# A mixture of experts: from every token through every expert to tokens sorted into 23 tiles of one expert each

## The chip, the cores and the metric

The kernel runs on one core of one Trainium2 chip. The metric is the device time of the program in microseconds (us). A core has TensorE (PE, matrix products), VectorE (DVE), ScalarE (ACT), GpSimd (POOL), SyncE (SP, here the issuer of DMAs), the on-chip memories SBUF and PSUM, and 16 DMA engines between SBUF and DRAM.

## The reference, cut to what matters

Two layers work on x of 2048 tokens of 128 values. The change touches only the last part, a mixture of experts with eight experts (H = 128, F = 512), of which each token wants the result of one:

```
hn2    = layernorm(x) * g + b                       # (2048, 128)
logits = hn2 @ gate_w + gate_b                      # (2048, 8)
idx    = argmax(logits, axis=-1)                    # one expert per token
mid    = relu(einsum('th,ehf->etf', hn2, w1) + b1[:, None, :])
y      = einsum('etf,efh->eth', mid, w2) + b2[:, None, :]
moe    = y[idx, arange(2048)]
return x + moe
```

All numbers are float32.

## The kernel before, in words

The program is a chain of stages, each a block in which every engine has its own list of instructions; `end_stage` frees the semaphores and lets all engines meet at a barrier. The two stages of the mixture come last, and after them one DMA writes the result (L1564).

`moe_prep_stage` normalises the 16 groups of 128 tokens (`xn`), transposes them on TensorE (L1413), scales and shifts them into `hn2` on ScalarE, forms the logits (L1418), and VectorE works out the one-hot choice `oh` (L1393 to L1401). TensorE then transposes `oh` (L1424) and multiplies it by `b2` (L1430), and VectorE adds that to the residual `S.res` (L1406).

`moe_stage` runs every token through every expert: 8 experts times 4 chunks of 512 tokens are 32 steps. A step has four products of 512 tokens with `w1` (`hidden`, L1508), four ScalarE relus (L1478), 16 products of 128 tokens with `w2` (`output`, L1517) and four VectorE instructions (L1491) that add the result times the column of `oh` to `S.res`, so that only the chosen expert counts. SyncE loads an expert's weights (256 KB for `w1`, 256 KB for `w2`, 2 KB for `b1`) into one of two buffers, two experts ahead. Nothing leaves SBUF until the end.

The order on each engine is the order in which the code is written; semaphores are the only link between engines. A float32 product on TensorE with a 128 x 128 weight shows as two matmul rows in the profile, a transpose as one.

Of the kernel before, what the change touches and what calls it, by code (L numbers as in the profile page):

```python
# [14 lines left out]
I32 = mybir.dt.int32  # L15
ALU = mybir.AluOpType
# [3 lines left out]
P = 128  # L20
# [12 lines left out]
NFB = NF // P  # L33
DI, NS, KC, DR = 256, 16, 4, 8
# [1283 lines left out]
def moe_prep_stage(nc, S, dr):  # L1318

    with ExitStack() as ctx:  # L1320
# [22 lines left out]
        @block.sync  # L1343
        def _(sp):
            sp.dma_start(gw[:, :], dr["gate_w"]).then_inc(w_load, 16)
            sp.dma_start(gb[:, :], dr["gate_b"]).then_inc(w_load, 16)
            sp.dma_start(b2[:, :], dr["b2"]).then_inc(w_load, 16)
            sp.wait_ge(w_load, 48)

        @block.gpsimd  # L1350
        def _(pool):

            pool.iota(rank_i[:, :], pattern=[[-1, NE]], base=NE, channel_multiplier=0).then_inc(rank_ready, 1)

        @block.scalar
        def _(act):
            act.wait_ge(var_ready, 1)
            act.activation(lnv[:, :], lnv[:, :], ACT.Ln).then_inc(act_c, 1)
            act.wait_ge(act_c, 1)
            act.activation(rstd[:, :], lnv[:, :], ACT.Exp, scale=-0.5).then_inc(rstd_ready, 1)  # L1360
            for c in range(NCH):
                act.wait_ge(xn_psum, c + 1)
                act.activation(S.hn2[:, c * CH:(c + 1) * CH], banks[c], ACT.Identity, bias=V("ln2_b"),
                               scale=V("ln2_g")).then_inc(hn_ready, 1)
            for c in range(NCH):
                act.wait_ge(ohT_psum, c + 1)
                act.activation(ohT[:, c * CH:(c + 1) * CH], banks[c][0:NE, :], ACT.Copy).then_inc(ohT_ready, 1)

        @block.vector
        def _(dve):  # L1370
# [18 lines left out]
            dve.wait_ge(rank_ready, 1)  # L1389
            link(dve.tensor_copy(rank[:, :], rank_i[:, :]))  # L1390
            dve.wait_ge(w_load, 48)
# [6 lines left out]
            link(dve.tensor_tensor(pick[:, :, :], pick[:, :, :], rank[:, :].unsqueeze(1).to_broadcast([P, NT, NE]),  # L1398
                                   ALU.mult))
            link(dve.tensor_reduce(top[:, :], pick[:, :, :], AX.X, ALU.max))  # L1400
            dve.tensor_tensor(S.oh[:, :, :], pick[:, :, :], top[:, :].unsqueeze(2).to_broadcast([P, NT, NE]),  # L1401
                              ALU.is_equal).then_inc(oh_ready, 1)
            for c in range(NCH):
                dve.wait_ge(b2_psum, c + 1)
                r = S.res[:, TPC * c:TPC * (c + 1), :]
                dve.tensor_tensor(r, r, banks[4 + c].rearrange("p (i d) -> p i d", d=P), ALU.add).then_inc(dve_c, 1)  # L1406

        @block.tensor
        def _(pe):
# [5 lines left out]
            pe.wait_ge(w_load, 48)  # L1415
            pe.wait_ge(hn_ready, NCH)
            for t in range(NT):
                mm = pe.matmul(banks[4][:, NE * t:NE * (t + 1)], S.hn2[:, P * t:P * (t + 1)], gw[:, :],  # L1418
                               start=True, stop=True)
            mm.then_inc(lg_psum, 1)  # L1420
            pe.wait_ge(oh_ready, 1)
            for c in range(NCH):
                for i in range(TPC):
                    mm = pe.transpose(banks[c][0:NE, P * i:P * (i + 1)], S.oh[:, TPC * c + i, :], S.ident[:, :])  # L1424
                mm.then_inc(ohT_psum, 1)
            for c in range(NCH):
                pe.wait_ge(ohT_ready, c + 1)
                for i in range(TPC):
                    t = TPC * c + i
                    mm = pe.matmul(banks[4 + c][:, P * i:P * (i + 1)], ohT[:, P * t:P * (t + 1)], b2[:, :],  # L1430
                                   start=True, stop=True)
                mm.then_inc(b2_psum, 1)


def moe_stage(nc, S, dr):

    with ExitStack() as ctx:
# [5 lines left out]

        w1, w2, b1 = sb("w1", [P, 2, NF]), sb("w2", [P, 2, NFB, P]), sb("b1", [P, 2, NFB])
        mid = sb("mid", [P, 2, NFB, CH])
        banks = S.banks
        w_load = [sem("w_load0"), sem("w_load1")]
        mid_psum, mid_ready, y_psum, added = sem("mid_psum"), sem("mid_ready"), sem("y_psum"), sem("added")
        block = ctx.enter_context(nc.Block())
        NP = NE // 2  # L1450

        @block.sync
        def _(sp):
            def load(e, par):
                sp.dma_start(w1[:, par, :], dr["w1"][bass.ds(e, 1)].rearrange("o h f -> h (o f)")).then_inc(w_load[par], 16)  # L1455
                sp.dma_start(w2[:, par, :, :], dr["w2"][bass.ds(e, 1)].rearrange("o (b p) h -> p (o b) h", p=P))\  # L1456
                    .then_inc(w_load[par], 16)
                sp.dma_start(b1[:, par, :], dr["b1"][bass.ds(e, 1)].rearrange("o p b -> p (o b)")).then_inc(w_load[par], 16)

            load(0, 0)  # L1460
            load(1, 1)
            with sp.Fori(0, NP - 1) as ep:
                for par in range(2):

                    sp.wait_ge(y_psum, ep * (2 * NCH) + (NCH * (par + 1) + 2))
                    load(ep * 2 + (2 + par), par)

        @block.scalar
        def _(act):
            with act.Fori(0, NP) as ep:  # L1470
                for par in range(2):
                    for c in range(NCH):
                        step = NCH * par + c

                        act.wait_ge(y_psum, ep * (2 * NCH) + (step + 1))
                        for f in range(NFB):
                            act.wait_ge(mid_psum, ep * (2 * NCH * NFB) + (NFB * step + f + 1))
                            act.activation(mid[:, c % 2, f, :], banks[f], ACT.Relu,  # L1478
                                           bias=b1[:, par, f:f + 1]).then_inc(mid_ready, 1)

        @block.vector
        def _(dve):
            dve.sem_inc(added, 2)
            with dve.Fori(0, NP) as ep:
                for par in range(2):
                    for c in range(NCH):
                        step = NCH * par + c
                        dve.wait_ge(y_psum, ep * (2 * NCH) + (step + 3))
                        for i in range(TPC):
                            t = TPC * c + i  # L1490
                            ins = dve.scalar_tensor_tensor(  # L1491
                                out=S.res[:, t, :], in0=banks[4 + c % 2][:, P * i:P * (i + 1)],
                                scalar=S.oh[:, t, bass.ds(ep * 2 + par, 1)], in1=S.res[:, t, :],
                                op0=ALU.mult, op1=ALU.add)
                        ins.then_inc(added, 1)
                        dve.wait_ge(added, ep * (2 * NCH) + (step + 3))

        @block.tensor
        def _(pe):
            pe.sem_inc(mid_ready, NFB)  # L1500
            pe.sem_inc(y_psum, 2)

            def hidden(ep, par, c):
                step = NCH * par + c
                for f in range(NFB):

                    pe.wait_ge(mid_ready, ep * (2 * NCH * NFB) + (NFB * step + f + 1))
                    pe.matmul(banks[f], w1[:, par, P * f:P * (f + 1)], S.hn2[:, c * CH:(c + 1) * CH],  # L1508
                              start=True, stop=True).then_inc(mid_psum, 1)

            def output(ep, par, c):
                step = NCH * par + c
                pe.wait_ge(added, ep * (2 * NCH) + (step + 1))
                pe.wait_ge(mid_ready, ep * (2 * NCH * NFB) + (NFB * (step + 2)))
                for i in range(TPC):
                    for f in range(NFB):
                        mm = pe.matmul(banks[4 + c % 2][:, P * i:P * (i + 1)], mid[:, c % 2, f, P * i:P * (i + 1)],  # L1517
                                       w2[:, par, f, :], start=(f == 0), stop=(f == NFB - 1))
                mm.then_inc(y_psum, 1)

            with pe.Fori(0, NP) as ep:
                for par in range(2):
                    for c in range(NCH):
                        if c == 0:
                            pe.wait_ge(w_load[par], ep * 48 + 48)
                        hidden(ep, par, c)
                        if par or c:
                            output(ep, *divmod(NCH * par + c - 1, NCH))
                output(ep, 1, NCH - 1)
# [92 lines left out]
```

## Time and profile before

| | |
|---|---|
| device time, median of 3 runs | 1865.42 us (1864.46 to 1867.36) |
| the profiled execution: its own time | 1863.32 us |
| its span, first to last instruction | 1861.5 us |
| preparation stage, first instruction to last | 1588.93 to 1622.22 us |
| expert stage, first weight load issued to last add | 1622.99 to 1855.74 us |
| last DMA, issue to end of span | 1856.62 to 1861.5 us |

The profiled execution's time is 1.8 us more than its span; a change of the span is added to that time. Lines of the profile name lines of the kernel (L1508), and tiles by their names without buffer numbers, so that `xe_w` is both `w1` and `w2`, and `x_hn` is `hn2`.

### The profile page before, as it was taken

The page shows a single profiled execution, that of the slowest core. Times are in us where ns is not written, and L with a number is a line of the kernel's source. Part 1 is how long each engine was busy: PE and PEld are TensorE (multiplying, and loading weights), DVE is VectorE, ACT ScalarE, POOL GpSimd, SP SyncE. Part 2 cuts the span into 40 slices and gives each one's busy share as a digit, 9 for nine tenths or more (in the row PEclk, how much of TensorE's full clock was granted, in tenths as well). Part 3 has the DMA queues.
Part 4 walks back from the last instruction along what each step waited for, and adds up shares of the span by engine and source line. Part 5 has one row for each costly group of instructions (what it writes and reads, how often), then busy time and mean ns, then how long its engine had stood idle before and what let it go on. Part 6 is the DMA issues. An engine that isn't in the chain of part 4 may idle for free. (4 is left out here: it accounts for less than half of the span.)

```text
span 1861.5 us, 19912 instructions
## 1 busy us (share of the span) xinstructions
PE 1271.1 (68%) x6752; PEld 472.7 (25%) x6752; DVE 1273.2 (68%) x1980; ACT 892.9 (48%) x1211; POOL 476.7 (26%) x433
## 2 busy tenths in 40 slices
PE   0432599999999999999690233349223334699998
PEld 0220022222222222222230000023000002467776
DVE  8934899999999999994301899960179997311111
ACT  2220077777777777778443344423434442244332
POOL 1200000000000000000002999940279996000000
PEclk6765599999999999999895555569555555699999
DMA  0011010001000000000006655500565560000000
GB/s 27 0 76 73 28 48 1 2 34 41 1 1 38 38 2 1 2 1 1 22 4 175 131 114 112 102 10 15 148 132 113 111 131 4 23 12 23 11 23 23
DMA packets 53271, 86.33 MB, mean 46 GB/s; under 512 B 7950, under 2 KB 18854, under 8 KB 53182
## 3 DMA queue, kind: packets, MB, share of 16 engines
q1 hardware_dynamic: 53182, 85.23, 18.6%
q8 instruction: 46, 0.75, 0.2%
q14 instruction: 43, 0.35, 0.1%
HBM read 71.81 MB, written 13.11 MB: 46 GB/s over the span
## 5 line engine op out<-in xcount | busy, mean ns | idle before, releaser
L653 DVE TENSOR_REDUCE at_mpart<-psum 128x1 f32<-128x512 f32 x1024 | 656.8, 686 | 48.5 <-PE psum L718 37.6
L632 ACT ACTIVATE at_probs<-psum 128x1024 f32<-128x1024 f32 x512 | 496.2, 1021 | 272.3 <-PE psum L743 272.1
L756 PE MATMUL psum<-at_probs,at_vg 128*32 128x512 f32 x2048 | 273.6, 606 | 0.4 <-ACT at_probs L632 0.4
L743 PE MATMUL psum<-at_qs,at_ks 75*128 75x512 bf16 x1024 | 269.7, 385 | 1.3 <-ACT at_probs L632 0.2
L714 PE MATMUL psum<-at_ks,at_qs 64*128 64x512 bf16 x512 | 207.9, 406 | 84.2 <-DMA at_km<-k_parts 49.9
L718 PE MATMUL psum<-at_km,at_qm 64*128 64x512 bf16 x512 | 208.0, 406 | 0.0
L608 POOL CAST at_m<-at_mneg 128x16 bf16<-128x16 f32 x16 | 3.1, 196 | 697.8 <-DVE at_mneg L658 697.8
L1491 DVE SCALAR_TENSOR_TENSOR res<-psum,x_oh,res 128x128 f32<-128x128 f32 x128 | 36.0, 344 | 197.5 <-PE psum L1517 197.5
L1239 PE MATMUL psum<-msf_hc,m_stack 128*32 128x512 f32 x256 | 60.1, 1027 | 161.1 <-DVE msf_hc L1164 151.9
L1239 PE MATMUL psum<-msb_hc,m_stack 128*32 128x512 f32 x256 | 59.9, 1024 | 160.8 <-DVE msb_hc L1164 151.8
L1220 POOL TENSOR_TENSOR msb_inject<-msb_dus,msb_bs 128x512 f32<-128x512 f32 x128 | 160.6, 1319 | 26.9 <-DMA msb_cs<-m_bc 26.9
L1220 POOL TENSOR_TENSOR msf_inject<-msf_dus,msf_bs 128x512 f32<-128x512 f32 x128 | 159.7, 1299 | 27.2 <-DMA msf_cs<-m_bc 27.2
L1478 ACT ACTIVATE xe_mid<-psum,xe_b 128x512 f32<-128x512 f32 x128 | 87.9, 687 | 145.1 <-PE psum L1508 145.1
L714 PEld LDWEIGHTS psum<-at_ks,at_qs 64*128 64x128 bf16 x512 | 47.7, 93 | 384.3 <-DVE at_mpart L653 331.1
L1517 PEld LDWEIGHTS psum<-xe_w,xe_mid 128*128 128x128 f32 x1024 | 118.8, 192 | 13.4 <-issue 13.4
L1508 PE MATMUL psum<-x_hn,xe_w 128*128 128x512 f32 x256 | 117.6, 606 | 5.5 <-DMA xe_b<-in_b 5.5
L1517 PE MATMUL psum<-xe_w,xe_mid 128*128 128x128 f32 x1024 | 118.8, 275 | 0.0
L743 PEld LDWEIGHTS psum<-at_qs,at_ks 75*128 75x128 bf16 x1024 | 78.2, 98 | 135.4 <-issue 52.0
L1148 ACT ACTIVATE psum<-msf_dts,m_aneg 128x512 f32<-128x512 f32 x128 | 85.5, 686 | 47.4 <-DVE msf_hp L1191 19.1
L1148 ACT ACTIVATE psum<-msb_dts,m_aneg 128x512 f32<-128x512 f32 x128 | 85.5, 686 | 47.0 <-DVE msb_hp L1191 19.1
L1191 DVE TENSOR_TENSOR_SCAN psum<-psum,msf_last,msf_inject 128x512 f32<-128x512 f32 x66 | 84.6, 1318 | 0.0
L1191 DVE TENSOR_TENSOR_SCAN psum<-psum,msb_last,msb_inject 128x512 f32<-128x512 f32 x66 | 84.3, 1313 | 0.0
(240 smaller groups left out, 1311.4 us busy)
## 6 DMA issues: line engine op xcount, KB each, us to landing
msf_dts<-m_dt SPq DMA_DIRECT2D x32, 256.0 KB
msf_dus<-m_dtu SPq DMA_DIRECT2D x32, 256.0 KB
msb_dts<-m_dt SPq DMA_DIRECT2D x32, 256.0 KB
msb_dus<-m_dtu SPq DMA_DIRECT2D x32, 256.0 KB
at_qs<-q_parts SPq DMA_DIRECT2D x48, 96.0 KB
at_ks<-k_parts SPq DMA_DIRECT2D x48, 96.0 KB
msf_bs<-m_bc SPq DMA_DIRECT2D x16, 256.0 KB
msf_cs<-m_bc SPq DMA_DIRECT2D x16, 256.0 KB
```

What stands on the lines that cost most here:

```text
L632: act.activation(probs[:, u % 2, p, :], s_pair[p], ACT.Exp, scale=float(HD) ** -0.5).then_inc(probs_ready, 1)
L653: dve.reduce_max(mpart[:, s % 2, 2 * jp + b, i, kc:kc + 1], ring[x % 3], AX.X).then_inc(ring_free, 1)
L714: pe.matmul(ring[x % 3], S.qs[0:HALF, buf, q], S.ks[0:HALF, buf, k], start=True, stop=True)\
L718: pe.matmul(ring[y % 3], S.qm[64:64 + HALF, buf, q], S.km[64:64 + HALF, buf, k], start=True, stop=True)\
L743: mm = pe.matmul(s_banks[p][b], S.ks[0:DM, g % 2, j * T + kt * P:j * T + (kt + 1) * P], S.qs[0:DM, g % 2, j * T + c * CH:j * T + (c + 1) * ...
L756: mm = pe.matmul(o_bank[VW * j:VW * (j + 1), :], vg[:, g % 2, kt, j, :], probs[:, u % 2, j // 2, CH * (j % 2):CH * (j % 2 + 1)], start=(kt ...
L1148: act.activation(decay[k % ND], dts[:, i % 2, j, :], ACT.Exp, scale=S.aneg[:, n:n + 1]).then_inc(decay_ready, 1)
L1191: dve.tensor_tensor_scan(h, decay[k % ND], inject[:, k % NI, :], before if c else 0.0, ALU.mult, ALU.add).then_inc(scanned, 1)
L1220: pool.tensor_tensor(inject[:, k % NI, :], dus[:, i % 2, j, :], bs[:, c % 2, q, :], ALU.mult).then_inc(injected, 1)
L1239: mm = pe.matmul(y_bank[i % 2][GC * j:GC * (j + 1), :], S.stack[:, :], hc[:, r % 2, j, :], start=False, stop=(q == NQ - 1), tile_position= ...
L1508: pe.matmul(banks[f], w1[:, par, P * f:P * (f + 1)], S.hn2[:, c * CH:(c + 1) * CH], start=True, stop=True).then_inc(mid_psum, 1)
L1517: mm = pe.matmul(banks[4 + c % 2][:, P * i:P * (i + 1)], mid[:, c % 2, f, P * i:P * (i + 1)], w2[:, par, f, :], start=(f == 0), stop=(f == ...
```

## The change

The expert stage no longer takes every token through every expert. The preparation stage works out, for each token, a row in a list sorted by expert, in which each expert starts at a new tile of 128 rows; `NSLOT` = 16 + 8 - 1 = 23 tiles hold any choice. The normalised tokens are scattered to `x_dram` in DRAM, one indirect DMA on POOL's queue for each of the 16 groups; before that a plain DMA fills `x_dram` with zeros. The product of the one-hot choice with `b2` is gone from this stage. `eid` is the expert of each tile. The expert stage then walks over the 23 tiles: SyncE loads the tile's 128 rows of `x`, reads the expert's number from SBUF into a register, and loads `w1`, `b1`, `w2` and `b2` from that expert's address (`W` = 3 buffers); TensorE transposes `x`, multiplies by `w1`, then a row of ones by `b2` and the hidden values by `w2`; ScalarE evicts; SyncE stores the 128 result rows to `y_dram`. When all 23 are stored, POOL gathers them by 16 indirect DMAs, and VectorE adds them to `S.res`. The loops over experts are now written out.

The core of the diff (declarations, and lines that only rename, are left out):

```diff
@@ moe_prep_stage, sync @@
-            sp.dma_start(b2[:, :], dr["b2"]).then_inc(w_load, 16)
-            sp.wait_ge(w_load, 48)
+            sp.wait_ge(zeros_ready, 1)
+            sp.dma_start(S.x_dram.rearrange("(s p) d -> p s d", p=P),
+                         zeros[:, :].unsqueeze(1).to_broadcast([P, NSLOT, P])).then_inc(zeroed, 16)
+            sp.wait_ge(w_load, 32)
@@ gpsimd @@
+            pool.wait_ge(zeroed, 16)
+            pool.wait_ge(pos_ready, 1)
+            for i in range(NT):
+                pool.indirect_dma_start(S.x_dram, bass.IndirectOffsetOnAxis(ap=S.pos[:, i:i + 1], axis=0),
+                                        xn[:, i, :], None).then_inc(scattered, 16)
+            pool.wait_ge(scattered, 16 * NT)
@@ scalar @@
-            for c in range(NCH):
-                act.wait_ge(ohT_psum, c + 1)
-                act.activation(ohT[:, c * CH:(c + 1) * CH], banks[c][0:NE, :], ACT.Copy).then_inc(ohT_ready, 1)
@@ vector @@
-            for c in range(NCH):
-                dve.wait_ge(b2_psum, c + 1)
-                r = S.res[:, TPC * c:TPC * (c + 1), :]
-                dve.tensor_tensor(r, r, banks[4 + c].rearrange("p (i d) -> p i d", d=P), ALU.add).then_inc(dve_c, 1)
+            dve.wait_ge(counts, 1)
+            link(dve.tensor_tensor_scan(upto[:, :, :].rearrange("p e i -> p (e i)"),
+                                        first[:, :, :].rearrange("p e i -> p (e i)"), of_tile, 0.0, ALU.mult, ALU.add))
...
+            link(dve.tensor_reduce(posf[:, :], rank[:, :, :].rearrange("p e i -> p i e"), AX.X, ALU.add))
+            dve.tensor_copy(S.pos[:, :], posf[:, :]).then_inc(pos_ready, 1)
...
+            link(dve.tensor_copy(S.eid[:, :], eidf[:, :]))
@@ tensor @@
-            for c in range(NCH):
-                for i in range(TPC):
-                    mm = pe.transpose(banks[c][0:NE, P * i:P * (i + 1)], S.oh[:, TPC * c + i, :], S.ident[:, :])
...
-                    mm = pe.matmul(banks[4 + c][:, P * i:P * (i + 1)], ohT[:, P * t:P * (t + 1)], b2[:, :],
-                                   start=True, stop=True)
+            pe.matmul(banks[5][:, 0:NE * NT], before[:, :], chosen, start=True, stop=True)
+            pe.matmul(banks[6][:, 0:NE * NT], every[:, :], chosen, start=True, stop=True).then_inc(counts, 1)
@@ moe_stage, sync @@
+            def load(s):
+                w = s % W
+                if s >= W:
+                    sp.wait_ge(y_psum, s - W + 1)
+                sp.dma_start(x[:, w, :], S.x_dram[P * s:P * (s + 1), :]).then_inc(loaded[w], 16)
+                e = sp.value_load(S.eid[0:1, s:s + 1], min_val=0, max_val=NE - 1)
+                sp.dma_start(w1[:, w, :], dr["w1"][bass.ds(e, 1)].rearrange("o h f -> h (o f)")).then_inc(loaded[w], 16)
+                sp.dma_start(b1[:, w, :], dr["b1"][bass.ds(e, 1)].rearrange("o p b -> p (o b)")).then_inc(loaded[w], 16)
+                sp.dma_start(w2[:, w, :, :], dr["w2"][bass.ds(e, 1)].rearrange("o (b p) h -> p (o b) h", p=P))\
+                    .then_inc(loaded[w], 16)
+                sp.dma_start(b2[:, w, :], dr["b2"][bass.ds(e, 1)]).then_inc(loaded[w], 16)
+            def store(s):
+                sp.wait_ge(y_ready, s + 1)
+                sp.dma_start(S.y_dram[P * s:P * (s + 1), :], y[:, s % 2, :]).then_inc(stored[s % 2], 16)
+            for s in range(NSLOT):
+                load(s)
+                if s >= 2:
+                    store(s - 2)
+            store(NSLOT - 2)
+            store(NSLOT - 1)
@@ gpsimd @@
+            pool.wait_ge(stored[0], 16 * ((NSLOT + 1) // 2))
+            pool.wait_ge(stored[1], 16 * (NSLOT // 2))
+            for i in range(NT):
+                pool.indirect_dma_start(moved[:, i, :], None, S.y_dram,
+                                        bass.IndirectOffsetOnAxis(ap=S.pos[:, i:i + 1], axis=0)).then_inc(gathered[i // TPC], 16)
@@ scalar @@
+            turn(0)
+            for s in range(NSLOT):
+                if s + 1 < NSLOT:
+                    turn(s + 1)
+                act.wait_ge(mid_psum, s + 1)
...
+                for f in range(NFB):
+                    act.activation(mid[:, s % 2, f, :], m_bank[s % 2][:, P * f:P * (f + 1)], ACT.Relu,
+                                   bias=b1[:, s % W, f:f + 1]).then_inc(mid_ready, 1)
+                if s >= 1:
+                    out(s - 1)
+            out(NSLOT - 1)
@@ vector @@
+            for c in range(NCH):
+                dve.wait_ge(gathered[c], 16 * TPC)
+                r = S.res[:, TPC * c:TPC * (c + 1), :]
+                dve.tensor_tensor(r, r, moved[:, TPC * c:TPC * (c + 1), :], ALU.add).then_inc(added, 1)
@@ tensor @@
+            def turn(s):
+                pe.wait_ge(loaded[s % W], 16 * 5 * (s // W + 1))
...
+                pe.transpose(t_bank[s % 2][:, 0:P], x[:, s % W, :], S.ident[:, :]).then_inc(turned, 1)
+            def output(s):
...
+                pe.matmul(y_bank[s % 2][:, 0:P], ones[:, :], b2[:, s % W, :], start=True, stop=False)
+                for f in range(NFB):
+                    pe.wait_ge(mid_ready, NFB * s + f + 1)
+                    mm = pe.matmul(y_bank[s % 2][:, 0:P], mid[:, s % 2, f, :], w2[:, s % W, f, :],
+                                   start=False, stop=(f == NFB - 1))
+                mm.then_inc(y_psum, 1)
+            turn(0)
+            for s in range(NSLOT):
+                if s + 1 < NSLOT:
+                    turn(s + 1)
+                pe.wait_ge(xT_ready, s + 1)
...
+                for f in range(NFB):
+                    mm = pe.matmul(m_bank[s % 2][:, P * f:P * (f + 1)], w1[:, s % W, P * f:P * (f + 1)], xT[:, s % 2, :],
+                                   start=True, stop=True)
+                mm.then_inc(mid_psum, 1)
+                if s >= 1:
+                    output(s - 1)
+            output(NSLOT - 1)
```

`turn(s)` of ScalarE takes the transposed tile out of PSUM with scale and shift (`xT`), and `out(s)` waits for `y_psum` of s and copies the result into `y` (`y_ready`).

On SyncE, in the expert stage before, the loads of one expert inside the loop (w1, w2 and b1 are the weight buffers; ISA and REGISTER_ALU rows set registers):

```order
L1455 ISA
L1455 DMA xe_w1<-in_w1 128x512
L1456 DMA xe_w2<-in_w2 128x4x128
L1458 ISA
L1458 DMA xe_b1<-in_b1 128x4
L1465 REGISTER_ALU
```

On SyncE in the expert stage now, one tile in the steady part (x_done is `y_dram`, x_rows is `x_dram`):

```order
L1518 DMA x_done<-xe_y 128x128
L1508 DMA xe_x<-x_rows 128x128
L1509 TENSOR_LOAD x_eid
L1509 ISA x2
L1510 ISA
L1510 DMA xe_w1<-in_w1 128x512
L1511 ISA
L1511 DMA xe_b1<-in_b1 128x4
L1512 DMA xe_w2<-in_w2 128x4x128
L1514 ISA
L1514 DMA xe_b2<-in_b2 1x128
```

The store of an earlier tile stands ahead of the load of the next one, and the register load stands between the load of `x` and the weights.

On TensorE in the expert stage now, from its start to the first steady tile (L1578 is the transpose in `turn`, L1599 `hidden`, L1583 and L1586 `output`):

```order
L1578 MATMUL psum<-ident,xe_x 128x128 x2
L1599 MATMUL psum<-xe_xT,xe_w1 128x128 x4
L1578 MATMUL psum<-ident,xe_x 128x128
L1599 MATMUL psum<-xe_xT,xe_w1 128x128 x4
L1583 MATMUL psum<-xe_b2,xe_ones 128x128
L1586 MATMUL psum<-xe_w2,xe_mid 128x128 x4
```

The transpose of the tile after the present one comes first in each turn of the loop, then `hidden` of the present tile, then `output` of the one before; before the change TensorE had here, for each step, 4 products of 512 columns and 16 of 128.

On POOL, in the preparation stage and in the expert stage now (before there was one IOTA, L1353):

```order
L1376 AFFINE_SELECT xp_before<-xp_every 128x128
L1381 DMA x_rows<-xp_xn,x_pos 2944x128 x16
L1325 UNCONDITIONAL_BRANCH
L58 ISA
L1527 UNCONDITIONAL_BRANCH
L1529 MEMSET xe_ones 1x128
L1533 DMA xe_moved<-x_done,x_pos 128x128 x16
```

The 16 scatters end the preparation stage, and the 16 gathers end the expert stage.

## Rows read from the trace of the kernel before

**Rows 1.** Windows: stretch, length, busy (x) per engine, clock, DMA share, GB/s.

```profile
1622.99:1626.96 3.97, 0.00 (x0) 0.00 (x1) 0.00 (x0) 0.00 (x0) 0.00 (x0) 0.50 0.71 211
1655.00:1855.70 200.70, 199.47 (x1152) 146.02 (x1150) 33.61 (x120) 76.94 (x112) 0.00 (x0) 1.00 0.06 16
```

**Rows 2.** Groups by line and shape, 1500 us to the end: busy, mean | idle before.

```profile
L1517 PE MATMUL psum<-xe_w,xe_mid 128*128 128x128 f32 x1024 | 118.8, 275 | 0.0
...
L1508 PE MATMUL psum<-x_hn,xe_w 128*128 128x512 f32 x256 | 117.6, 606 | 5.5 <-DMA xe_b<-in_b 5.5
L1478 ACT ACTIVATE xe_mid<-psum,xe_b 128x512 f32<-128x512 f32 x128 | 87.9, 687 | 145.1 <-PE psum L1508 145.1
```

**Rows 3.** Timeline of SyncE, DMA issues from 1560 us on.

```profile
1572.48 0.39 SPq L1259 DMA_DIRECT2D mob_w<-in_w_out  x1
...
1622.99 0.34 SPq L1455 DMA_DIRECT2D xe_w<-in_w  x1
...
1623.86 0.50 SPq L1458 DMA_DIRECT2D xe_b<-in_b  x1
...
1686.49 0.33 SPq L1455 DMA_DIRECT2D xe_w<-in_w  x1
...
1687.49 0.36 SPq L1458 DMA_DIRECT2D xe_b<-in_b  x1
```

**Rows 4.** Timeline, end of the program.

```profile
1854.61 1.13 DVE L1491 SCALAR_TENSOR_TENSOR res<-psum,x_oh,res 128x128 f32<-128x128 f32 x4 [2.45 <-PE psum L1517]
1856.62 0.40 SPq L1564 DMA_DIRECT2D out<-res  x1
```

**Rows 5.** Timeline, TensorE after a load, 1560 to 1590 us.

```profile
1574.66 9.22 PE L1269 MATMUL psum<-mob_w,m_zs 128*128 128x128 f32 x64 [3.71 <-DMA mob_w<-in_w_out]
```

**Rows 6.** Timeline (start us, length us), preparation stage 1590 to 1623 us.

```profile
1595.15 0.21 ACT L1360 ACTIVATE xp_rstd<-xp_lnv 128x16 f32<-128x16 f32 x1
...
1596.57 4.19 PE L1413 MATMUL psum<-ident,xp_xn 128*128 128x128 f32 x16 [9.26 <-DVE xp_xn L1387]
...
1599.51 0.17 DVE L1390 CAST xp_rank<-xp_rank_i 128x8 f32<-128x8 int32 x1
...
1608.84 0.29 DVE L1393 TENSOR_TENSOR xp_lg<-psum,xp_gb 128x128 f32<-128x128 f32 x1 [9.16 <-PE psum L1418]
1609.16 0.29 DVE L1395 TENSOR_REDUCE xp_top<-xp_lg 128x16 f32<-128x128 f32 x1
...
1610.46 0.29 DVE L1401 TENSOR_TENSOR x_oh<-xp_pick,xp_top 128x128 f32<-128x128 f32 x1
...
1614.31 7.19 PE L1430 MATMUL psum<-xp_b,xp_ohT 8*128 8x128 f32 x32
...
1621.53 0.69 DVE L1406 TENSOR_TENSOR res<-res,psum 128x512 f32<-128x512 f32 x1 [1.02 <-PE psum L1430]
```

**Rows 7.** Windows, TensorE alone: four stretches, busy (x), granted clock, DMA, GB/s.

```profile
1500.00:1520.00 20.00, 5.69 (x28) 0.50 0.71 145
1614.30:1621.60 7.30, 7.20 (x33) 0.50 0.00 0
1626.90:1633.00 6.10, 6.04 (x7) 0.50 0.14 38
1633.00:1640.50 7.50, 7.50 (x42) 0.99 0.01 2
```

**Rows 8.** Waits of SyncE's queue: total, times, longest.

```profile
SPq L1320 <- DMA xp_b<-in_b: 1.7, 1, 1.7
```

**Rows 9.** Timeline, first product of the expert stage.

```profile
1626.96 10.16 PE L1508 MATMUL psum<-x_hn,xe_w 128*128 128x512 f32 x16 [5.46 <-DMA xe_b<-in_b]
```

**Rows 10.** DMA issues: count, KB each, us from issue to landing.

```profile
m_bc<-mpf_bcx SPq DMA_DIRECT2D x4, 64.0 KB, 1.6
```

**Rows 11.** Groups, POOL, whole program.

```profile
L1220 POOL TENSOR_TENSOR msb_inject<-msb_dus,msb_bs 128x512 f32<-128x512 f32 x128 | 160.6, 1319 | 26.9 <-DMA msb_cs<-m_bc 26.9
```

**Rows 12.** Groups, VectorE, 1500 us to the end.

```profile
L1191 DVE TENSOR_TENSOR_SCAN psum<-psum,msb_last,msb_inject 128x512 f32<-128x512 f32 x29 | 37.4, 1331 | 0.0
```

More of the change, by code:

```diff
@@ L15 @@
 I32 = mybir.dt.int32
+U32 = mybir.dt.uint32
 ALU = mybir.AluOpType
@@ new lines, in _ @@
+            link(dve.tensor_tensor(full[:, :, :], upto[:, :, NT - 1:NT].to_broadcast([P, NE, NT]),
+                                   steps[:, :].unsqueeze(1).to_broadcast([P, NE, NT]), ALU.is_gt))
+            link(dve.tensor_reduce(tiles[:, :], full[:, :, :], AX.X, ALU.add))
+            link(dve.tensor_tensor_scan(ends[:, :], every[:, 0:NE], tiles[:, :], 0.0, ALU.mult, ALU.add))
+            link(dve.tensor_tensor(starts[:, :], ends[:, :], tiles[:, :], ALU.subtract))
+            link(dve.tensor_scalar(starts[:, :], starts[:, :], float(P), None, ALU.mult))
@@ new lines, in moe_stage @@
+        mid, y = sb("mid", [P, 2, NFB, P]), sb("y", [P, 2, P])
+        ones = sb("ones", [1, P])
+        moved = sb("moved", [P, NT, P])
+        t_bank, m_bank, y_bank = S.banks[0:2], S.banks[2:4], S.banks[4:6]
+        loaded = [sem(f"loaded{w}") for w in range(W)]
+        stored = [sem("stored0"), sem("stored1")]
+        gathered = [sem(f"gathered{c}") for c in range(NCH)]
+        turned, xT_ready, mid_psum, mid_ready, y_psum, y_ready = (sem("turned"), sem("xT_r"), sem("mid_psum"), sem("mid_r"),
+                                                                  sem("y_psum"), sem("y_r"))
@@ L1449, in moe_stage, with V @@
+        ones_ready, added = sem("ones_r"), sem("added")
         block = ctx.enter_context(nc.Block())
-        NP = NE // 2
+        def V(n):
+            return S.vec[:, VCOL[n]:VCOL[n] + 1]
         @block.sync
         def _(sp):
[L1454 to L1466, printed above, removed]
+            def load(s):
[18 more added lines that the diff above has]
+            store(NSLOT - 1)
@@ L1521, in _, with turn @@
[L1521 to L1529, printed above, removed]
+            def turn(s):
+                pe.wait_ge(loaded[s % W], 16 * 5 * (s // W + 1))
+                if s >= 2:
+                    pe.wait_ge(xT_ready, s - 1)
+                pe.transpose(t_bank[s % 2][:, 0:P], x[:, s % W, :], S.ident[:, :]).then_inc(turned, 1)
@@ L1532, in moe @@
+            output(NSLOT - 1)
 def moe(nc, S, dr):
     with ExitStack() as ctx:
-        S.hn2 = ctx.enter_context(nc.sbuf_tensor("x_hn2", [P, T], F32))
-        S.oh = ctx.enter_context(nc.sbuf_tensor("x_oh", [P, NT, NE], F32))
+        S.pos = ctx.enter_context(nc.sbuf_tensor("x_pos", [P, NT], U32))
+        S.eid = ctx.enter_context(nc.sbuf_tensor("x_eid", [P, NSLOT], I32))
+        S.x_dram, S.y_dram = (nc.dram_tensor(f"x_{n}", [NSLOT * P, P], F32).ap() for n in ("rows", "done"))
         moe_prep_stage(nc, S, dr)
```

137 lines of the change are left out of this document (72 added, 65 removed).

## The prediction

> **What bounds the kernel now.** I read the windows first, then the groups, then the timelines at both ends of the two last stages. From 1655 to 1855.7 us TensorE is busy 199.47 of 200.70 us at the full granted clock, and the DMA engines are 6% busy [rows 1]. So the expert stage is TensorE's own work. The groups divide it nearly evenly: 118.8 us for `output` and 117.6 us for `hidden`, while ScalarE's relus take 87.9 us and wait 145.1 us for TensorE [rows 2]. Tokens per product are what costs here: the 1024 rows of `output` are 512 products (two rows each), 0.232 us a product of 128 tokens at the full clock [rows 2]. The stage runs from the first load issued at 1622.99 us [rows 3] to the last add, 1854.61 + 1.13 = 1855.74 us; the last DMA is issued 0.88 us later, at 1856.62, and the span ends 4.88 us after that [rows 4]. That is 232.75 us of stage. In the new kernel the same arithmetic is an eighth plus padding: 23 tiles with 1 transpose and 9 products each. At 0.232 us that would be about 50 us. The question is whether the rest of a tile hides behind it, and this is read from the code's order before any row.
>
> **One turn of the new loop.** TensorE's turn s is: transpose of tile s+1, `hidden` of s, `output` of s-1. The transpose waits for all five loads of s+1. On SyncE these stand behind the store of s-2, which waits for `out(s-2)` on ScalarE, which waits for `output(s-2)`, the last thing in TensorE's turn s-1. So the load that the next turn begins with is only issued when the present turn has ended: nothing is prefetched after the first three tiles, whatever `W` says of buffers. The period is a loop of four legs in series.
>
> *TensorE.* The clock decides the price. A load after idle shows matmuls starting at 1574.66 us [rows 5]. In the preparation stage, 16 transposes take 4.19 us, 0.26 us each, and the 16 products of L1430 take 7.19 us [rows 6], 0.45 us each, at a granted clock of 0.50, the lower level, 1.2 GHz [rows 7]. A stretch with TensorE busy 5.69 of 20 us stays at 0.50, and the first steps of the old expert stage do so for 6.1 us of unbroken work before the clock is at 0.99 [rows 7]. The new turn is a burst of about 4 us followed by a gap, so I take the lower level: 0.26 + 9 x 0.45 = 4.31 us. At the full clock it would be about 0.14 + 9 x 0.232 = 2.23 us.
>
> *ScalarE.* From TensorE's end to the next engine's start 0.15 us, and one eviction of 128 columns. 16 columns take 0.21 us [rows 6] and 512 take 0.687 us [rows 2]; in proportion, 0.31 us. The relus of the tile end before `output` does. With 0.1 us to SyncE: 0.56 us.
>
> *SyncE.* In the old loop w1 and b1 are issued 1.00 us apart [rows 3] with one DMA and one ISA row between, and issues take 0.33 to 0.50 us: I take 0.45 us per DMA with its gap and 0.14 per ISA. The leg has 6 DMAs (the store, x, w1, b1, w2, b2) and 5 ISAs: 2.7 + 0.7 = 3.4 us. The register load TENSOR_LOAD has no row. It is at least an ISA row, 0.15 us, and at most a whole small DMA, issued and landed, 0.33 + 1.7 = 2.0 us [rows 8]. It reads memory, so it lies well above the first: 1.0 us. Sum 4.4 us. One sentence on a price that only a page has: the Trainium skill ("DMA: Bandwidth & Descriptors", Latency and other measured facts) gives a floor of about 600 ns for a tensor load, by which the estimate would be 0.4 us less per tile, 9 us in all; no row here shows it.
>
> *Landing.* The first product of the old stage starts at 1626.96 us [rows 9], 2.6 us after b1's issue ended (1623.86 + 0.50 [rows 3]) and with a second expert in flight; 4 KB alone take 1.7 us [rows 8]; mob_w, 128 KB, starts TensorE 1.8 us after its issue ended [rows 3, 5]. Between 1.7 and 2.6 us I take 2.2, and 0.05 to TensorE. Bandwidth isn't the limit: the stretch of the first loads ran at 211 GB/s [rows 1], by which the 0.59 MB of a tile need 2.8 us, most of it under the issues.
>
> The period is 4.31 + 0.56 + 4.4 + 2.25 = 11.5 us; bounds 2.23 + 0.56 + 3.55 + 1.75 = 8.1 and 4.31 + 0.56 + 5.4 + 2.65 = 12.9.
>
> **The whole expert stage.** The first three loads are 3 x 3.95 = 11.85 us of issue, then 2.2: TensorE transposes tile 2 at 14.1 us. 20 periods bring tile 22: 230 us. Behind that come one turn (4.31), `hidden` of 22 (1.8), two `outputs` (4.5), eviction and store issue 1.0, and the landing, 1.6 us as for the 64 KB writes [rows 10]: 13.2. Together 257 us to the last store landed. Then POOL's 16 gathers. An indirect DMA has no row. Below it is a SyncE issue, 0.43 us. Above, an issue with its landing, 2.0 us. The work is to walk over 128 offsets on POOL; the nearest row is POOL's own pass over 128 partitions, 1.32 us [rows 11], so 1.3. 16 x 1.3 = 20.8, landing 2.2, an add of 0.69 [rows 6]: 23.7 us.
>
> **The preparation stage.** Up to `oh`, ending 1610.75 us, nothing changes. Removed is the rest up to 1622.22 [rows 6], the 16 transposes, 4 copies, 16 products and adds: 11.5 us. Added: two products, 0.9 us, and 0.2 us of hand-over; then 12 linked VectorE instructions up to `pos`. Seven of 128 columns at 0.29, four small at 0.17 [rows 6], and a scan between 0.29 and the 1.33 us of 512 columns [rows 12], say 0.37, with 0.03 us between linked ones: 3.5 us, ending 1615.4. Then 16 scatters, 20.8 us, landing 2.2, and the 0.77 us from 1622.22 to the next stage's first issue. The stage after starts at 1639.2 instead of 1622.99: +16.2 us. The `eid` chain (four instructions) lies under the scatters, the zero fill of 1.5 MB (7 us at 211 GB/s, issued near 1590) under the layer norm; without that cover they would cost 1 and 7 us. POOL's constants lie under the layer norm too.
>
> **The sum.** 1639.2 + 257 + 23.7 + 0.88 + 4.88 = 1925.7 us of span against 1861.5: +64. With the profiled execution's own 1863.3 us this is 1927.5, and the median lies 2.1 us above that execution: about 1928 to 1930. I say 1928. By stages: the expert stage +24 up to its last store plus +24 for the gathers, the preparation +16.
>
> On the indirect DMAs a rule stands against the change. The Trainium skill ("DMA: Bandwidth & Descriptors", Anatomy of one DMA) puts a DMA from the GpSimd queue at about 2.0 us plus bytes by bandwidth, mostly completion; as latency it agrees with the 2.2 us landing used here, and no row shows it for an indirect one. If it were paid 32 times in series at 2.15 us instead of 1.3, this estimate would be 27 us more, 1955 us.
>
> **Rivals.**
> 1. *Full clock* (12%). If the bursts hold TensorE at 2.4 GHz, each turn loses 2.1 us: 20 x 2.1 + 5 = 47 us, 1881 us, still slower. For it: the clock did rise after 6.1 us of work [rows 7]. Against: bursts of 4 us with gaps of 7. The Trainium skill ("TensorE: Matmul & The Clock Gate", Part 1) says that activity releases the clock and idleness throttles it again; the row of the stretch at 0.50 agrees.
> 2. *The load leg is short* (10%), the other side. Place: SyncE's list and the landing, 6.65 us of the period. With all other terms as they are, the change pays from a period of 11.5 - 64/20 = 8.3 us on, that is when this leg is 3.4 us. If the loads ran ahead after all, the period would be the 4.9 us of TensorE and ScalarE, and the time 1928 - 20 x 6.6 = 1796 us. Against it: the five loads and the wait stand in one list in this order, and an issue has never been below 0.33 us.
> 3. *Indirect DMAs in series* (10%): each issued only when the one before has landed, 1.3 + 2.2 = 3.5 us each; 32 x 2.2 = +70, 1998 us.
> My forecast, latency in series at the low clock, has 68%.
>
> **Range.** Ends of the unknown costs at once: a period of 8.1 and indirect DMAs of 0.43 us give 1823; 12.9 and 2.0 give 1983. Both ends together are unlikely; full clock (1881) belongs inside, the series rival outside. 1875 to 1985 leaves out about 2 in 10. No change from the median is what a measurement here can't tell apart, 0.2%, 3.7 us. Faster needs rival 2 or most cheap ends at once: 12%. Within 0.2%: 2%. Slower: 86%.
>
> **What would show it.** In the new trace: TensorE's granted clock near 0.5 in the expert stage and its busy share about 35 to 40%; a period near 11.5 us between transposes L1578; the transposes waiting for the DMA into a load tile in nearly every turn; on SyncE the store's wait for ScalarE's `y` as the only long one; a gap of the length of a TENSOR_LOAD, about 1 us, between x and w1; 16 scatters in about 21 us and as much for the gathers, everything else idle. I am wrong if the transposes don't wait, if the clock is 1.0, or if the indirect DMAs take well over 2 us each.

## The result, and the profile after

The changed kernel takes 1920.63 us (median of 4 runs, 1917.06 to 1923.9) against 1864.94 us before (1861.57 to 1867.36): a ratio of 1.030, 95% interval 1.0275 to 1.0324, slower by 3%. The profiled execution's span is 1919.4 us.

In the windows of the new trace, TensorE alone (length, busy (x), granted clock, DMA share, GB/s), the stretch that answers to the second of [rows 1] is this:

```profile
1655.00:1880.00 225.00, 97.97 (x381) 0.50 0.21 59
```

TensorE was busy 199.47 of 200.70 us at a clock of 1.00; it is now busy 98 of 225 us at 0.50. Less arithmetic is left, and it runs at the lower of the clock's levels, with more than half of the time idle. The groups by line and shape, which answer to [rows 2], say who ends the idle time (busy, mean ns of one | idle before):

```profile
L1586 PE MATMUL psum<-xe_w,xe_mid 128*128 128x128 f32 x184 | 47.7, 441 | 0.0
L1599 PE MATMUL psum<-xe_xT,xe_w 128*128 128x128 f32 x184 | 44.0, 421 | 0.0
...
L1381 POOL DMA_INDIRECT x_rows<-xp_xn,x_pos x16 | 15.6, 975 | 31.2 <-DVE x_pos L1448 26.6 <-issue 4.6
L1533 POOL DMA_INDIRECT xe_moved<-x_done,x_pos x16 | 15.2, 950 | 255.6 <-DMA x_done<-xe_y 251.0 <-issue 4.6
...
L1578 PE MATMUL psum<-ident,xe_x 128*128 128x128 f32 x23 | 10.9, 473 | 164.5 <-DMA xe_b<-in_b 164.5
```

The two large groups have 184 rows each instead of 1024 and 256. The wait stands at the transpose L1578: 164.5 us of waiting for a load, 34.0 of it before the first tile, in a group that works for 10.9 us. One turn shows the loop. In the timeline (start us, length us), from the store of one tile to the store of the next:

```profile
1701.96 0.34 SPq L1518 DMA_DIRECT2D x_done<-xe_y  x1
1702.36 0.42 SPq L1508 DMA_DIRECT2D xe_x<-x_rows  x1
1703.71 0.35 SPq L1510 DMA_DIRECT2D xe_w<-in_w  x1
1704.24 0.34 SPq L1511 DMA_DIRECT2D xe_b<-in_b  x1
1704.69 0.38 SPq L1512 DMA_DIRECT2D xe_w<-in_w  x1
1705.25 0.28 SPq L1514 DMA_DIRECT2D xe_b<-in_b  x1
...
1707.88 0.47 PE L1578 MATMUL psum<-ident,xe_x 128*128 128x128 f32 x1 [6.26 <-DMA xe_b<-in_b]
...
1708.15 1.91 PE L1599 MATMUL psum<-xe_xT,xe_w 128*128 128x128 f32 x8
...
1709.99 0.79 PE L1583 MATMUL psum<-xe_b,xe_ones 1*128 1x128 f32 x2
...
1710.71 2.08 PE L1586 MATMUL psum<-xe_w,xe_mid 128*128 128x128 f32 x8
1712.83 0.28 ACT L1549 ACTIVATE xe_y<-psum 128x128 f32<-128x128 f32 x1 [1.58 <-PE psum L1586]
1713.13 0.34 SPq L1518 DMA_DIRECT2D x_done<-xe_y  x1
```

Read it downwards as one chain. SyncE issues the store (1701.96), x, then w1 only 1.35 us after x, for the register load stands between them, then b1, w2 and b2, whose issue ends at 1705.53. 2.35 us later, at 1707.88, TensorE begins the transpose that waited for the last of these. It works without a break until 1712.79, ScalarE evicts, and at 1713.13 the next store is issued. The loop took 11.17 us; from the first such store (1657.63) to the 20th (1871.67) the mean is 11.27 us. SyncE's own waits say the same from its side (total, times, longest):

```profile
SPq L1518 <- ACT xe_y L1549: 166.1, 23, 7.9
```

The preparation stage, timeline, against [rows 6]: the token positions are ready at 1615.94 us, and the 16 scatters follow.

```profile
1615.77 0.17 DVE L1448 CAST x_pos<-xp_posf 128x16 uint32<-128x16 f32 x1
...
1616.83 1.20 POOL L1381 DMA_INDIRECT x_rows<-xp_xn,x_pos  x1 [26.58 <-DVE x_pos L1448]
1618.33 0.96 POOL L1381 DMA_INDIRECT x_rows<-xp_xn,x_pos  x1 [0.30 <-issue]
...
1636.03 0.96 POOL L1381 DMA_INDIRECT x_rows<-xp_xn,x_pos  x1 [0.30 <-issue]
1640.56 0.33 SPq L1508 DMA_DIRECT2D xe_x<-x_rows  x1
```

They start 1.26 us apart, 0.96 us of work and 0.30 us of issue each (the first takes 1.20 us), and the next stage's first DMA is issued at 1640.56 us, 17.6 us later than the 1622.99 of [rows 3]. The gathers at the end, timeline, against [rows 4]:

```profile
1891.77 0.99 POOL L1533 DMA_INDIRECT xe_moved<-x_done,x_pos  x1 [251.01 <-DMA x_done<-xe_y]
1893.07 0.96 POOL L1533 DMA_INDIRECT xe_moved<-x_done,x_pos  x1 [0.30 <-issue]
...
1910.60 0.94 POOL L1533 DMA_INDIRECT xe_moved<-x_done,x_pos  x1 [0.30 <-issue]
1913.06 0.69 DVE L1570 TENSOR_TENSOR res<-res,xe_moved 128x512 f32<-128x512 f32 x1 [4.17 <-DMA xe_moved<-x_done,x_pos]
1914.53 0.39 SPq L1640 DMA_DIRECT2D out<-res  x1
```

From the last store's landing (1891.77) to the end of the last add (1913.75) are 22.0 us, in which TensorE, ScalarE and SyncE have nothing to do.

### The profile page after: what moved, and what is told of

The parts are those of the page before. It is cut to its first block and busy times, and to the rows that moved or that the text cites. A ratio compares the mean times of both kernels' runs of the same rounds, so it can differ in the third digit from the quotient of the medians.

```text
span 1919.4 us, 17941 instructions
## 1 busy us (share of the span) xinstructions
PE 1147.4 (60%) x5865; PEld 396.3 (21%) x5865; DVE 1241.1 (65%) x1870; ACT 846.0 (44%) x1217; POOL 509.1 (27%) x473
## 3 DMA queue, kind: packets, MB, share of 16 engines
q0 software_dynamic: 1024, 2.10, 0.4%
## 5 line engine op out<-in xcount | busy, mean ns | idle before, releaser
L1578 PE MATMUL psum<-ident,xe_x 128*128 128x128 f32 x23 | 10.9, 473 | 164.5 <-DMA xe_b<-in_b 164.5
L1542 ACT ACTIVATE xe_xT<-psum,vec 128x128 f32<-128x128 f32 x23 | 10.5, 457 | 178.8 <-PE psum L1578 178.8
L1533 POOL DMA_INDIRECT xe_moved<-x_done,x_pos x16 | 15.2, 950 | 255.6 <-DMA x_done<-xe_y 251.0
L1236 PE MATMUL psum<-m_u,m_diag 128*32 128x512 f32 x128 | 30.3, 1029 | 49.5 <-PEq L59 49.5
```

## The experiments

The series theory: in SyncE's list each load stands behind a store that needs the end of TensorE's present turn, so the legs of a tile add up. Its rivals: too few buffers, transfers as the bound, TensorE's clock as the only cost. In the experiments "series theory" means this, "period" the time from one tile to the next in the steady part, and "stage" the time from the first load of x to the first gather, 251.2 us in the changed kernel (1640.56 to 1891.77).

The ratios in brackets are to the kernel before, with the 95% interval. Up to the expert stage these kernels have the same code, yet their profiled executions begin that stage anywhere from 1636.38 (e5) to 1645.97 us (e3). So differences of a few us are read from medians of four executions or from the length of the stage, never from where one execution ends.

**e1_w4, the fourth buffer alone.**

```diff
-        W = 3
+        W = 4
```

> A fourth weight and x buffer (W = 4), nothing else. Series theory: the load of tile s+1 stands behind the store of s-2 in SyncE's list, so a free buffer is of no use; the period stays 11.2 us and the time 1920 us (within 4 us). Rival, too few buffers (the load waits for y_psum of the tile whose buffer it takes): a tile of slack appears, the period falls to about 5.6 us and the time to about 1808 us.

Measured: 1922.68 us (ratio to before 1.0315, 1.0289 to 1.034), no change against the changed kernel. In SyncE's timeline, the first line of a turn and of the next:

```profile
1701.46 0.34 SPq L1518 DMA_DIRECT2D x_done<-xe_y  x1
...
1712.82 0.34 SPq L1518 DMA_DIRECT2D x_done<-xe_y  x1
```

This turn takes 11.36 us, and the mean period is 11.27, as in the changed kernel. With this order of the list the free buffer is not used.

**e2_lag3, the order of the list alone.** Behind load s SyncE now stores tile s-3 instead of s-2, a lag of 3. The same edit with W = 4 and a lag of 3 is e3; with W = 6 and a lag of 5, e4.

```diff
+        LAG = 3
...
             for s in range(NSLOT):
                 load(s)
-                if s >= 2:
-                    store(s - 2)
-            store(NSLOT - 2)
-            store(NSLOT - 1)
+                if s >= LAG:
+                    store(s - LAG)
+            for s in range(NSLOT - LAG, NSLOT):
+                store(s)
```

> W = 3 as in the changed kernel, but the store of tile s-3 instead of s-2 follows load s in SyncE's list. Series theory: the load of s+1 now waits for output(s-2) alone and no longer for ScalarE's eviction (0.3 us) and the store's issue (0.4 us): 20 periods of about 10.5 us instead of 11.2, so 13 us less, about 1907 us. Rival, the order of the list is all that stands against prefetch: the period falls to about 5.6 us, 1808 us.

Measured: 1905.83 us (1.0218, 1.0195 to 1.0241), 15 us less than the changed kernel. In SyncE's timeline, a store and the load after it:

```profile
1702.84 0.34 SPq L1519 DMA_DIRECT2D x_done<-xe_y  x1
1710.10 0.33 SPq L1509 DMA_DIRECT2D xe_x<-x_rows  x1
```

The store now goes out early, and the load waits 6.9 us behind it for `output` of the tile whose buffer it takes. With three buffers the order alone gives back the eviction and the store's issue, no more: the mean period is 10.62 us. Neither edit alone makes a prefetch.

**e3_w4_lag3, both.**

> Both: W = 4, and the store of s-3 after load s. Series theory: a whole turn of slack for each load, two periods must hold the loop of 11.2 us, so 5.6 us a tile; the expert stage up to the last store lasts 139 us instead of 251, the time is about 1809 us, faster than the kernel before by 3%. Rival, transfers bound the tile (0.59 MB in rows of 512 bytes and 16 bytes): the period stays above 8 us and the time above 1860 us. Granted clock: if the denser products raise it, the period is 4.4 us and the time 1780 us.

Measured: 1810.66 us (0.9705, 0.9667 to 0.9742), 110 us less than the changed kernel and 3% faster than the kernel before. Timeline of TensorE, three transposes in a row, and two windows (length, busy, granted clock, DMA share, GB/s):

```profile
1686.81 0.47 PE L1579 MATMUL psum<-ident,xe_x 128*128 128x128 f32 x1 [0.44 <-DMA xe_b<-in_b]
...
1692.45 0.47 PE L1579 MATMUL psum<-ident,xe_x 128*128 128x128 f32 x1 [0.74 <-DMA xe_b<-in_b]
...
1697.93 0.47 PE L1579 MATMUL psum<-ident,xe_x 128*128 128x128 f32 x1 [0.57 <-DMA xe_b<-in_b]
```

```profile
1660.00:1720.00 60.00, 52.42 (x205) 0.50 0.42 114
1720.00:1740.00 20.00, 16.34 (x77) 0.63 0.38 106
```

The transposes are 5.64 and 5.48 us apart, half of the loop, as two tiles are in flight. Up to 1720 us the clock stays at 0.50. Behind that it rises late in some turns (the products of `output` that begin at 1728.57 us take 1.16 us instead of 2.08), and after the gap of 2.37 us that follows it is at the lower level again. The stage lasts 134.2 us, 117 less than in the changed kernel.

**e4_w6_lag5, loads as far ahead as SyncE can issue them.**

> W = 6 and the store of s-5 after load s: loads run as far ahead as SyncE issues them. Series theory: what bounds is now TensorE, 4.9 us a tile at the lower clock (125 us of stage, 1795 us); if the unbroken work raises the granted clock to 1.0, SyncE's issues of 3.6 us a tile bound, 92 us of stage, 1762 us. Rival, transfers: no gain over the run with four buffers.

Measured: 1764.01 us (0.9456, 0.9434 to 0.9478); once more as e11: 1765.31 us (0.9484, 0.9452 to 0.9515). Windows of TensorE:

```profile
1660.00:1680.00 20.00, 18.96 (x114) 0.81 0.64 175
1680.00:1700.00 20.00, 15.66 (x102) 0.91 0.61 175
1700.00:1720.00 20.00, 13.99 (x99) 1.00 0.64 177
```

The clock rose in the first of them, in the third turn that followed without a break. It fell for a turn in the second, and is 1.00 in the third with TensorE busy 14 of 20 us. While loaded tiles are in stock the turns are 2.5 us (1669.28 to 1671.78); from 1678.22 to 1731.28 us the stock is used up, and 14 tiles follow each other 3.79 us apart. SyncE's issues of the same tiles' x are 3.79 us apart too (1672.47 to 1725.52): mostly 3.62, with a few in which a single issue takes up to 1.3 us, for a reason that no run here shows. So SyncE's list is the bound. That transfers bounded e3 is refuted: the DMA share went from 0.42 there to 0.64, at 177 GB/s.

**e5_fixed, without the register load.** This kernel takes the weights of expert s mod 8 for tile s, whatever the tokens chose.

```diff
-                e = sp.value_load(S.eid[0:1, s:s + 1], min_val=0, max_val=NE - 1)
+                e = s % NE
```

> The changed kernel (W = 3) without the register load: tile s takes the weights of expert s mod 8 from a fixed address, so most tokens get another expert's result; all transfers keep their sizes. In the trace of the changed kernel w1 is issued 0.93 us after the end of x's issue, 0.9 us longer than between two plain DMAs. Theory (register load and its ISA rows are serial in the period): 0.9 us less a turn and also 0.4 us less of ISA rows ahead of b1 and b2, 20 periods of about 9.9 to 10.3 us, 1895 to 1902 us. Rival (the landing of x and the weights hides it): the landing leg grows by as much, the time stays at 1920 us.

Measured: 1899.77 us (1.0208, 1.018 to 1.0237), 21 us less than the changed kernel. SyncE's timeline:

```profile
1702.86 0.34 SPq L1518 DMA_DIRECT2D x_done<-xe_y  x1
1703.25 0.42 SPq L1508 DMA_DIRECT2D xe_x<-x_rows  x1
1703.72 0.43 SPq L1510 DMA_DIRECT2D xe_w<-in_w  x1
1704.19 0.43 SPq L1511 DMA_DIRECT2D xe_b<-in_b  x1
...
1712.95 0.34 SPq L1518 DMA_DIRECT2D x_done<-xe_y  x1
```

x to w1 is 0.47 us instead of 1.35. This turn takes 10.09 us, but the mean period is 10.37 us, 0.9 less than the 11.27 of the changed kernel and just outside the 9.9 to 10.3 expected: the further 0.4 us ahead of b1 and b2 did not come (w1 to the end of b2 takes 1.79 us in the turn from 1692.15, against 1.82). So the register load with the ISA rows behind it costs 0.88 us a tile. Over the 23 loads that is 20 us, and the stage is 20.4 us shorter: it is in series, as the theory has it.

**e6_filler, work for TensorE while it waits.** 20 products into a bank that nobody reads, at the end of each turn:

```diff
                 if s >= 1:
                     output(s - 1)
+                if 1 <= s <= NSLOT - 3:
+                    for _ in range(20):
+                        pe.matmul(S.banks[6][:, 0:P], S.ident[:, :], S.ident[:, :], start=True, stop=True)
```

> The changed kernel (W = 3) with 20 products of the identity by itself into an unused bank at the end of each of TensorE's turns 1 to 20, in the time in which it waits for the load. Nothing waits for their result. Theory (the tile's products cost 4.9 us because of the lower clock): with little idle time left the granted clock goes to 1.0, the turn's own products fall to about 2.5 us, the fillers take 4.6 us of the 6.3 us of waiting, and the period falls from 11.2 to about 8.8 us: 1872 us. Rival (the load leg hides what TensorE does, so its clock is of no matter): no less than 1920 us. If the clock doesn't rise, the fillers take 9 us a turn, longer than the wait, and the period is about 14 us, 1975 us.

Measured: 1893.35 us (1.0157, 1.0138 to 1.0176): faster than the changed kernel by 27 us, with 400 products more. The expectation of 49 us was too high: the mean period is 9.86 us, not 8.8. Timeline of TensorE (L1578 opens a turn, L1586 closes its work, L1606 is filler):

```profile
1726.13 0.33 PE L1578 MATMUL psum<-ident,xe_x 128*128 128x128 f32 x1 [0.28 <-DMA xe_b<-in_b]
...
1727.70 1.16 PE L1586 MATMUL psum<-xe_w,xe_mid 128*128 128x128 f32 x8
...
1728.69 4.63 PE L1606 MATMUL psum<-ident 128*128 128x128 f32 x40
...
1735.86 0.33 PE L1578 MATMUL psum<-ident,xe_x 128*128 128x128 f32 x1 [2.54 <-DMA xe_b<-in_b]
...
1737.85 2.08 PE L1586 MATMUL psum<-xe_w,xe_mid 128*128 128x128 f32 x8
```

The first turn shown runs at the full clock: 2.73 us from 1726.13 to the end of its last product, instead of 4.91. In the next one the clock fell in its midst (2.08 us for the same eight rows, not 1.16), after 2.54 us in which TensorE had waited. Over 1660 to 1740 us the granted clock was 0.84. Where the clock is low, the fillers also outlast the wait: those from 1739.72 us take 6.52 us instead of 4.63, and the next transpose follows them without waiting for its load. The clock is a term of the period, worth 2.2 us a tile, and the fillers hold it only part of the time.

**e7_halfrows, gathers of 64 rows.** Only partitions 0 to 63 get an expert's result, and POOL first clears the tile.

```diff
-                pool.indirect_dma_start(moved[:, i, :], None, S.y_dram,
-                                        bass.IndirectOffsetOnAxis(ap=S.pos[:, i:i + 1], axis=0))...
+                pool.indirect_dma_start(moved[0:64, i, :], None, S.y_dram,
+                                        bass.IndirectOffsetOnAxis(ap=S.pos[0:64, i:i + 1], axis=0))...
```

> The changed kernel (W = 3), in which each of the 16 gathers at the end fetches only the rows of partitions 0 to 63; the tokens of the other partitions get no expert result (POOL clears the tile early in the stage). Theory (an indirect DMA costs its issue, 1.25 us from start to start, and little by rows): the gathers still start 1.2 us apart, 1920 us. Rival (POOL's time goes by rows): they start 0.7 us apart, 9 us less, about 1911 us.

Measured by its timeline, from one run of 1927.61 us, in which the scatters had already started 5.2 us later than in the changed kernel, ahead of the edit, so that the total says nothing:

```profile
1899.32 0.91 POOL L1535 DMA_INDIRECT xe_moved<-x_done,x_pos  x1 [0.30 <-issue]
1900.53 0.90 POOL L1535 DMA_INDIRECT xe_moved<-x_done,x_pos  x1 [0.30 <-issue]
```

With half of the rows most of the gathers start 1.21 us apart instead of 1.25, and take 0.90 us instead of 0.95. Two of the 16 took 1.4 us, so that the whole series, 19.0 us from the first start to the last, is no shorter than the 18.8 of the changed kernel. Between 64 and 128 rows an indirect DMA costs by its number, hardly by its rows.

**e8_w6_actstore, the stores on ScalarE's queue.** W = 6, four y buffers (NY = 4), and SyncE's list has only loads; the two added lines stand behind the eviction in `out(s)`:

```diff
             for s in range(NSLOT):
                 load(s)
-                if s >= 2:
-                    store(s - 2)
...
+                act.wait_ge(y_ready, s + 1)
+                act.dma_start(S.y_dram[P * s:P * (s + 1), :], y[:, s % NY, :]).then_inc(stored[s % NY], 16)
```

> W = 6, SyncE only loads, ScalarE issues the store of a tile itself behind its eviction, four y buffers instead of two. Series theory after the run with six buffers: SyncE's list is the bound there (3.6 us a tile); without the store it is 3.2 us, and ScalarE no longer waits for stores: 20 x 0.4 us less, about 1755 us. Rival 1, bandwidth bounds (177 GB/s in that run): the same as with six buffers, 1764 us. Rival 2, the stores on ScalarE make it the bound (0.46 + 1.14 + 0.28 + 0.4 us and its waits, above 3.6 us): slower, 1770 us or more.

Measured: 1759.56 us (0.9437, 0.9421 to 0.9452), and as e10 1758.61 us (0.9429, 0.941 to 0.9449). Beside e10 on the same chip e11 had 1765.31 us: 7 us less. One window, in e8 and then in e10, which are the same kernel:

```profile
1665.00:1725.00 60.00, 53.85 (x341) 0.86 0.68 184
```

```profile
1665.00:1725.00 60.00, 51.58 (x370) 1.00 0.70 195
```

The clock differs between executions of one kernel: it is 0.86 in e8's profiled one, where the transposes stand 2.5 us apart in some stretches and 4.7 in others, and 1.00 in e10's; e4 and e11, again one kernel, have 0.95 and 0.91. So the comparison is that of the stage on one chip: 94.4 us in e11, 86.7 in e10. The issues of x are 3.64 and 3.27 us apart on average (all 23), and 22 times that difference is 8 us: the shorter list shows in nearly full size. e8's own stage, 92.2 us, has part of this lost to the lower clock.

**e9_merged, b1 in the rows of w1.** Otherwise the kernel of e8. The rows of w1 in DRAM have b1 behind them (516 values), a rearrangement of the inputs; four loads a tile.

```diff
-                sp.dma_start(b1[:, w, :], dr["b1"][bass.ds(e, 1)].rearrange("o p b -> p (o b)")).then_inc(loaded[w], 16)
...
+    out["w1"] = np.concatenate([out["w1"], out["b1"]], axis=2)
```

> As the run with ScalarE's stores and W = 6, and b1 lies behind each row of w1 in DRAM (rows of 516 values), so that a tile has four loads instead of five and the 16-byte rows are gone. Theory (SyncE's list bounds there): 0.53 us less a tile, 20 tiles: 10 us less, 1749 us. Rival 1 (the transfers bound, 200 GB/s at 76% busy): the bytes are the same; only the 128 packets of 16 bytes go; 1756 to 1760 us. Rival 2 (ScalarE's 2.5 us and TensorE's 2.5 us a tile in turn bound): the same, 1759 us.

Measured: 1747.51 us (0.9372, 0.9352 to 0.9391), the fastest, 11 us less than e10 beside it and 6.3% faster than the kernel before. Timelines: two transposes on TensorE, then two loads of x on SyncE:

```profile
1677.42 0.27 PE L1571 MATMUL psum<-ident,xe_x 128*128 128x128 f32 x1
...
1679.93 0.33 PE L1571 MATMUL psum<-ident,xe_x 128*128 128x128 f32 x1
```

```profile
1691.91 0.34 SPq L1508 DMA_DIRECT2D xe_x<-x_rows  x1
...
1694.60 0.34 SPq L1508 DMA_DIRECT2D xe_x<-x_rows  x1
```

TensorE's turn is 2.51 us while tiles are in stock, and SyncE's list 2.69 us: the two are nearly level. The stage is 76.1 us, 10.6 less than in e10, and 22 times the difference of the mean spacing of the issues of x (3.27 and 2.80 us) is 10.3. The clock is no rival here, as it was at 1.00 in e10 already, and the 238 GB/s that this run reaches from 1660 to 1680 us speak against transfers as the bound of e10, with some 200. They do not exclude it by themselves, since the 16-byte rows are gone too.

e10 and e11 repeat e8 and e4:

> The kernel of e8 once more on the same chip as its neighbours here, to tell 5 us from nothing: 1755 to 1762 us.

> The kernel of e4 once more on the same chip as its neighbours here: 1762 to 1768 us, 4 us more than with the stores on ScalarE if those are worth anything.

## Why the prediction was right, point by point

1. *No prefetch, four legs in series.* Right, and shown: the transposes wait in nearly every turn, and e1 to e3 show that order and buffers must change together. The period was put at 11.5 us and is 11.27. TensorE's busy share was put at 35 to 40% and is 44% (97.97 of 225 us), for the reason of point 2.
2. *TensorE's leg* was put at 4.31 us and is 4.91. The products of `output` came out longer than 0.45: L1583 and L1586 take 2.80 us for five, 0.72 of them for the one product with `b2`. The clock at the lower level was right (0.50), and e6 shows its price.
3. *ScalarE and hand-overs*: 0.56 us forecast; 0.34 from 1712.79 to 1713.13. The two hand-overs, for which the sum had 0.15 and 0.1, are 0.04 and 0.02.
4. *SyncE's leg*: 4.4 us forecast; 3.57 from 1701.96 to 1705.53. The DMAs were priced at 0.45 us each, and the register load at 1.0 with five ISA rows at 0.14; it is 1.35 us from x to w1, and w1 to the end of b2 is 1.82. The Trainium skill's floor for a tensor load ("DMA: Bandwidth & Descriptors", Latency and other measured facts; about 600 ns), which the prediction gave beside its own 1.0, is the nearer: from the end of x's issue to w1 are 0.93 us, of which three ISA rows at 0.14 leave some 0.5 for the load, an estimate. An issue is also shorter than the 0.33 us that the prediction took as the least: that of b2 takes 0.28.
5. *Landing*: 2.25 us forecast; 2.35 here and 2.45 a turn later. Of the legs TensorE's was 0.60 us too short, SyncE's 0.83 and ScalarE's 0.22 too long, the landing 0.10 too short. That the sum is off by only 0.35 us a turn is luck: the mechanism was right, the single prices less so.
6. *Expert stage to the last store landed*: 257 us forecast; 1640.56 to 1891.77 is 251.2.
7. *Scatters and gathers*: 1.3 us each forecast; 1.26 and 1.25 measured, and e7 shows that the nearest row, a pass of POOL over 128 partitions, was near by chance: half of the partitions cost nearly as much. The gathers' end was put at 23.7 us and took 22.0.
8. *Preparation*: +16.2 us forecast, +17.6 measured; the scatters began 0.89 us after `pos`, for which the sum had no term. What fills that time is not shown.
9. *The sum*: 1925.7 us of span forecast, 1919.4 measured; 1928 against 1920.6 us. The expert stage of point 6 makes up these 6 us; points 7 and 8 nearly cancel.

Of the rivals, the full clock didn't come by itself (0.50 throughout), the short load leg wasn't there (3.57 + 2.35 = 5.9 us, not 3.4), and the indirect DMAs weren't in series with their landings: the scatters start 1.26 us apart, and a landing comes 2.2 us after its issue (median). The prediction's counterfactual, 1796 us if loads ran ahead, lies between what e3 and e4 gave, 1811 and 1764 us. It kept the lower clock; what it did not see is that denser work can then raise it, from which e4 has its further gain.

## What to carry to other kernels

Count buffers and read the issuing engine's list together: a load that stands behind a store in one list waits for that store's producer, however many buffers are free, and moving the load forward is of no use without a buffer to put it in. Each of the two edits alone was worth 0 to 15 us here, both together 110. When arithmetic is cut to under a fifth (184 rows instead of 1024 here), price the new loop by its serial legs (issue, landing, compute, eviction), and take TensorE's time at the clock that it will have when it waits, not at the one that it had. What sorting costs at both ends is a number of indirect DMAs, 1.25 us each: 40 us in this kernel that no run here removed. Whether part of the scatters could run beside the first loads was not tried.

## What the runs showed of the hardware

- The granted clock is 0.50 in e3 from 1660 to 1720 us, with TensorE busy 52.4 of 60 us in turns with a break before most of them (0.4 to 1.0 us in the steady turns). In e4 it rose to 1.00 by 1668 us, after work without a break from 1656.55 us, and was still there from 1700 to 1720 us, with TensorE busy 14.0 of 20.
- The length of a single break does not tell when it falls: in e4 it stayed at 1.00 behind a break of 1.57 us (ending 1682.52) and fell in the turn behind one of 1.54 us (ending 1689.96). Two executions of one kernel differ, 0.86 and 1.00 over the same 60 us (e8, e10). What decides between them is not shown.
- A register load from SBUF on SyncE with its three ISA rows costs 0.88 us in the list (1.35 against 0.47 us from x to w1).
- An indirect DMA on POOL costs 0.95 us and 0.30 us before the next, for 128 rows of 512 bytes, and mostly 0.90 us for 64 rows; they follow each other without waiting for the landing.
- SyncE's issue of six DMAs and a register load, 3.62 us in most tiles of e4, is above TensorE's work on a 128-token tile at the full clock, 2.5 us (e9).
